# A slot-attention stage rebuilt: all sixteen batches per iteration, the recurrent cell by four, context rows streamed

## The reference, cut to what matters

```python
Pn = rmsnorm(P, input_norm_w)                 # P: the context
k_proj, v_proj = Pn @ Wk.T, Pn @ Wv.T
for _ in range(3):                            # NUM_ITERS
    sn = rmsnorm(slots, slot_norm_w)
    q_proj = sn @ Wq.T
    scores = einsum('bkd,bmd->bkm', q_proj, k_proj) * SCALE
    attn = softmax(scores, axis=-2)           # over the 56 slots
    attn = attn / (sum(attn, axis=-1) + EPS)  # over the 1500 rows
    updates = einsum('bkm,bmd->bkd', attn, v_proj)
    slots = gru_cell(updates, slots, ...)     # r, z by sigmoid, candidate by tanh
```

## Time and profile before

| | us |
|---|---|
| median of three runs | 933.5 |
| profiled execution | 936.72 |
| its span | 934.9 |
| PE busy in the span | 813.6 (87%) |
| PEld busy | 573.1 (61%) |
| DVE busy | 618.5 (66%) |
| ACT busy | 561.9 (60%) |
| POOL busy | 449.7 (48%) |

### The profile page before, as it was taken

The page is one execution under the profiler, slowest core; times in us unless marked ns, Lnnn a source line. Parts: engine busy times, 40 slices in busy tenths (PEclk is TensorE's granted clock), DMA queues, the critical chain, the costliest instruction groups (busy, mean ns, idle before and its releaser), DMA issues.

```text
span 934.9 us, 24802 instructions
## 1 busy us (share of the span) xinstructions
PE 813.6 (87%) x9152; PEld 573.1 (61%) x9152; DVE 618.5 (66%) x1210; ACT 561.9 (60%) x1222; POOL 449.7 (48%) x568
## 2 busy tenths in 40 slices
PE   5788999999999999986606899999999997599997
PEld 2254666666666666642303788899989897245443
DVE  4875777777777777614684476777677775475663
ACT  3264666666666666640442667877777875255554
POOL 1869576666666676000040135553255552066665
PEclk8798999999999999996757689999899998599999
DMA  5325444443444442201331000003320002112200
GB/s 185 84 73 167 113 132 122 124 116 117 120 121 122 120 121 50 73 2 46 99 96 49 1 2 3 2 4 99 98 71 2 2 2 68 35 35 68 68 1 20
DMA packets 44612, 66.22 MB, mean 71 GB/s; under 512 B 4964, under 2 KB 30500, under 8 KB 44532
## 3 DMA queue, kind: packets, MB, share of 16 engines
q1 hardware_dynamic: 44536, 65.21, 24.2%
HBM read 46.30 MB, written 0.46 MB: 50 GB/s over the span
## 4 chain that ended last, share of the span: by engine, by line
PE 54%; DVE 15%; POOL 15%; issue 9%; ACT 3%; DMA 2%; SPq 1%; POOLq 0%; DVEq 0%; ACTq 0%
PE ps L1220 7%; POOL ctx_lo L576 7%; PE ps L1438 7%; PE ps L1250 7%; PE ps L1237 6%; PE ps L1425 5%; PE ps L1207 3%; PE ps L1196 3%; DVE tile_max L811 2%; PE ps L1330 2%; PE ps L1254 2%; PE ps L1184 1%; POOL rs_y L566 1%; POOL rs_a L562 1%; PE ps L1175 1%
## 5 line engine op out<-in xcount | busy, mean ns | idle before, releaser
L811 DVE TENSOR_REDUCE tile_max<-ps 128x1 f32<-128x500 f32 x336 | 214.6, 674 | 74.6 <-PE ps L1220 73.9
L599 ACT ACTIVATE probs<-ps 125x896 f32<-125x896 f32 x192 | 176.1, 917 | 106.7 <-PE ps L1237 106.3
L724 ACT ACTIVATE c_prob<-ps,c_bias,row_scale 125x56 f32<-125x56 f32 x576 | 176.6, 416 | 7.2 <-DVE c_bias L1043 7.0
L1220 PE MATMUL ps<-k_hi,qdiag 128*128 128x500 f16 x336 | 130.9, 392 | 12.2 <-DVE tile_max L811 11.0
L552 POOL TENSOR_TENSOR c_prob<-c_prob,c_weight 125x672 f32<-125x672 f32 x48 | 63.0, 1312 | 155.8 <-DVE c_weight L1057 154.9
L1425 PE MATMUL ps<-query_hi,ctx_hi 128*125 128x56 f16 x576 | 109.0, 223 | 2.4 <-ACT c_prob L724 1.7
L1425 PE MATMUL ps<-query_hi,ctx_lo 128*125 128x56 f16 x576 | 110.1, 224 | 0.0
L1425 PE MATMUL ps<-query_lo,ctx_hi 128*125 128x56 f16 x576 | 110.0, 224 | 0.0
L1237 PE MATMUL ps<-qstack,kstack 98*125 98x224 f16 x768 | 108.3, 263 | 0.4 <-issue 0.2
L576 POOL TENSOR_TENSOR ctx_lo<-ctx_hi,ctx_lo 128x448 f16<-128x448 f32 x64 | 71.9, 1124 | 70.7 <-ACT ctx_lo L770 70.7
L1237 PEld LDWEIGHTS ps<-qstack,kstack 98*125 98x125 f16 x768 | 86.7, 138 | 20.0 <-issue 5.7
(11 more groups left out here) (217 smaller groups left out, 1680.3 us busy)
## 6 DMA issues: line engine op xcount, KB each, us to landing
ctx<-in_ctxT SPq DMA_DIRECT2D x16, 750.0 KB, 5.2
rows_in<-in_ctx_rows SPq DMA_DIRECT2D x16, 750.0 KB
kstack<-k_hi SPq DMA_DIRECT2D x128, 93.8 KB, 2.7
ctx_rows<-in_ctx_rows SPq DMA_DIRECT2D x16, 750.0 KB
kstack<-k_lo SPq DMA_DIRECT2D x64, 93.8 KB, 2.7
ctx_hi<-in_wg SPq DMA_DIRECT2D x8, 256.0 KB, 2.7
ctx_hi<-in_wu SPq DMA_DIRECT2D x8, 256.0 KB, 3.0
ctx_hi<-in_wd SPq DMA_DIRECT2D x8, 256.0 KB, 3.7
```

The costliest lines, as they stand in the source:

```text
L599: nc.scalar.activation(probs[c % 3][0:CH, :].rearrange("p (k w) -> p k w", k=2), score_tile(c)[0:CH], ACT.Exp, scale=float(HD) ** -0.5 / W ...
L724: last = nc.scalar.activation(c_prob[b % 4][:, c, :], ps[0:CH, 2 * (b % 2) + c // 6, bass.ts(c % 6, TOK)], ACT.Exp, bias=c_bias[b % 2][:, ...
L811: nc.vector.reduce_max(tile_max[:, u % MAXT, u // MAXT:u // MAXT + 1], ps[:, MAXB + (u + p) % 2, 0:KCOLS], AX.X).then_inc(max_done, 1)
L1220: nc.tensor.matmul(ps[:, MAXB + (u + p) % 2, 0:KCOLS], qdiag[p][:, bass.ts(t, 128)], k_hi[p][:, bass.ts(j, KCOLS)], start=True, stop=True) ...
```

## The change

The third block is restructured.

- The halves go. Each iteration runs over all 16 batches (`UNITS_C` is now 48, numbered straight through), and all loops of the stage are written out.
- The hops are for a **group of four** batches (`QUAD`, 12 groups) instead of a pair. Their tiles are 224 columns wide (`QT`) instead of 112. `update_sums` stays by pairs and stands twice per group; the root uses four spread matmuls and 128 partitions.
- The offsets are new: a group has 16 units, 64 slots, from one iteration to the next, and its last hop stands at slot 59.
- The score matmuls load 128 columns instead of 125, by reading three columns past the chunk (`ctx_hi_flat`, `ctx_lo_flat`, with `PAD` columns at the end); the three extra rows of the result are not used.
- `c_prob` has six buffers instead of four; two of them lie in memory that held weights.
- `ctx_rows` has ten tiles: four batches stay (`RESIDENT`), the other twelve are streamed through six tiles in every iteration (`STREAMED`). The source is a padded copy in DRAM, 128 rows of 12 x 129 values, contiguous per partition. In all 40 loads instead of 16, each with the norm's column rewritten by GpSimd behind it.
- The candidate and the hidden part of the gates stay in PSUM (`new_cand`, `hidden_in`) instead of going through `gru_t`.

The core of the diff:

```diff
-        TENSOR_AT = dict(sums=15, turn=18, gates=19, means=24, spread=30, project=30)
-        SCALAR_AT = dict(copy=15, tanh=16, cand=18, hi=26)
-        VECTOR_AT = dict(rows=14, hidden=19, slots=20, root=24, normed=27, lo=28)
-        POOL_AT = dict(root=19)
+        TENSOR_AT = dict(spread=55, project=59, sums=(19, 27), turn=31, gates=39, means=47)
+        SCALAR_AT = dict(copy=28, tanh=36, cand=39, hi=54)
+        VECTOR_AT = dict(rows=27, hidden=39, slots=41, root=45, normed=53, lo=57)
+        POOL_AT = dict(root=40)
...
+        def streamed_load(n):
+            it, b = divmod(n, BATCH)
+            return it * (BATCH - RESIDENT) + b - RESIDENT
...
-            for b in range(BATCH // 2):
-                sp.dma_start(ctx_rows[:, b, :, 0:D], dram["ctx_rows"][b]).then_inc(rows_loaded[b], 16)
...
+            def slot_rows(n):
+                sp.dma_start(ctx_rows_all[:, rows_of(n)], dram["ctx_rows_wide"][n % BATCH]).then_inc(rows_loaded[rows_of(n)], 16)
...
+            for b in range(RESIDENT):
+                slot_rows(b)
+            sp.wait_ge(x2_done, 2)
+            streamed = [n for n in range(UNITS_C) if n % BATCH >= RESIDENT]
+            for i, n in enumerate(streamed):
+                if i >= STREAMED:
+                    sp.wait_ge(u_ready, streamed[i - STREAMED] // 2 + 1)
+                slot_rows(n)
...
+                it, b = divmod(n, BATCH)
+                if it == 0 or b >= RESIDENT:
+                    pool.wait_ge(rows_loaded[rows_of(n)], rows_landed(n))
+                    nc.gpsimd.tensor_copy(ctx_rows[:, rows_of(n), :, D], row_sq[:, b, :]).then_inc(rms_col_done, 1)
...
+                nc.scalar.activation(new_cand, gru_t[:, 2, :], ACT.Tanh, bias=gru_b[:, 2:3]).then_inc(cand_done, 1)
...
-                        hi, lo = (x[:, batch, bass.ts(c, CH)] for x in (ctx_hi, ctx_lo))
...
-                            last = nc.tensor.matmul(ps[0:CH, 2 * (b % 2) + c // 6, bass.ts(c % 6, TOK)], l, r, start=(j == 0), stop=(j == 2))
...
+                    at = batch * CTX + c * CH
+                    hi, lo = (x[:, at:at + 128] for x in (ctx_hi_flat, ctx_lo_flat))
...
+                        last = nc.tensor.matmul(ps[:, 2 * (n % 2) + c // 6, bass.ts(c % 6, TOK)], l, r, start=(j == 0), stop=(j == 2))
```

More of the change, by code:

```diff
@@ L23 @@
 NCH = CTX // CH
+PAD = 4
 HEADS, HD = 16, 8
@@ L334, in queries_before, with quad, rows_of @@
-        def queries_before(half, it, pair):
-            return (half * (ITERS - 1) + it - 1) * PAIRS + pair + 1
+                    work(g)
+                if n < UNITS_C and unit_last:
+                    unit(n, k)
+        def quad(g):
+            return bass.ts(g % PER_IT, QT)
+        new_cand, hidden_in = (ps[:, GATES, bass.ts(i, QT)] for i in range(2))
+        def streamed_load(n):
+            it, b = divmod(n, BATCH)
+            return it * (BATCH - RESIDENT) + b - RESIDENT
+        def rows_of(n):
+            return n % BATCH if n % BATCH < RESIDENT else RESIDENT + streamed_load(n) % STREAMED
@@ new lines, in update_sums, with sums @@
+            def update_sums(pair):
+                def sums(g):
+                    m = 2 * g + pair
+                    pe.wait_ge(c_attended, 2 * m + 2)
+                    for n in (2 * m, 2 * m + 1):
+                        pe.wait_ge(rows_loaded[rows_of(n)], rows_landed(n))
+                    wait(pe, u_rows_done, g)
+                    for c in range(NCH):
+                        for j in range(2):
+                            n = 2 * m + j
+                            last = nc.tensor.matmul(ps[64 * j:64 * j + TOK, UPD, (D + 1) * pair:(D + 1) * (pair + 1)], c_prob[n % PROBS][:, c, :],
+                                                    ctx_rows[:, rows_of(n), c, :],
+                                                    start=(c == 0), stop=(c == NCH - 1), skip_group_check=True)
+                    last.then_inc(u_ready, 1)
+                return sums
@@ L1461, in slot_means @@
+            def slot_means(g):
+                pe.wait_ge(r_sq, g + 1)
+                wait(pe, qc_done, g)
+                for i in range(QUAD):
                     last = nc.tensor.matmul(ps[32 * i:32 * i + 32, QUERY, 0:TOK], ones_mean[:, 0:32], rms_sq[:, bass.ts(i, TOK)], start=True, stop=True)
                 last.then_inc(r_var, 1)
-            def spread_roots(m, k, half, pair):
-                pe.wait_ge(r_inv, 3 * k + 3)
-                wait(pe, r_slots, k)
-                for i in range(2):
-                    last = nc.tensor.matmul(ps[:, QUERY, 128 + TOK * i:128 + TOK * (i + 1)], spread[0:64, i, :], rs_y[:], start=True, stop=True)
-                last.then_inc(r_spread, 1)
@@ L1471, in project_slots, with spread_roots @@
-            def project_slots(m, k, half, pair):
-                pe.wait_ge(r_slots, k + 1)
-                wait(pe, qc_done, k)
-                nc.tensor.matmul(ps[:, QUERY, 256:256 + PT], to_query[:], slots_n, start=True, stop=True).then_inc(qc_ready, 1)
-            iterations(pe, unit_of, [(TENSOR_AT["sums"], False, update_sums), (TENSOR_AT["turn"], False, turn_updates), (TENSOR_AT["gates"], False, gate_sums),
-                                     (TENSOR_AT["means"], True, slot_means), (TENSOR_AT["spread"], True, spread_roots), (TENSOR_AT["project"], True, project_slots)])
+            def spread_roots(g):
+                pe.wait_ge(r_inv, 3 * g + 3)
+                wait(pe, r_slots, g)
+                for i in range(QUAD):
+                    last = nc.tensor.matmul(ps[:, QUERY, 64 + TOK * i:64 + TOK * (i + 1)], spread[:, i, :], rs_y[:], start=True, stop=True)
+                last.then_inc(r_spread, 1)
@@ new lines, in project_slots @@
+            def project_slots(g):
+                pe.wait_ge(r_slots, g + 1)
+                wait(pe, qc_done, g)
+                nc.tensor.matmul(ps[:, QUERY, 288:288 + QT], to_query[:], slots_n, start=True, stop=True).then_inc(qc_ready, 1)
+            iterations(unit, [
+                (TENSOR_AT["spread"], True, spread_roots), (TENSOR_AT["project"], True, project_slots),
+                (TENSOR_AT["sums"][0], False, update_sums(0)), (TENSOR_AT["sums"][1], False, update_sums(1)),
+                (TENSOR_AT["turn"], False, turn_updates), (TENSOR_AT["gates"], False, gate_sums), (TENSOR_AT["means"], True, slot_means)])
```

415 lines of the change are left out of this document (185 added, 230 removed).

## The result

The kernel after takes 880.96 us (median of 4 runs, 878.04 to 883.41) against 933.52 us of the kernel before in the same session. The ratio is 0.9448, with a 95% interval of 0.9400 to 0.9496: 52.6 us faster. The forecast was 897 us with a range from 872 to 925. The profiled execution of after took 883.04 us, its span 880.8 us.

The account below looks back on a forecast made before the run. Bound before: the cycle through GpSimd's root, beside TensorE's own load. Stage to last exponential 224.4 against 262.1 us, 37.7 less, minus 2 at its end: 36; 936.7 - 36 = 900.7, median 3.2 lower: 897 us, range 872 to 925.

Parts of the forecast that it names:

- the root cycle: Third block before: spread, score matmuls, GpSimd's root and the next pair's spread form a closed cycle, 10.74 us for two units.
- The score matmuls: TensorE, third block: with 128 columns loaded, steps fall from 57.5 to 33 ns, a unit's scores from 2.07 to 1.2 us.
- The sum to the last exponential: Third block, first to last exponential: ScalarE's exponentials, hops, waits and clock additions total 224.4 us against 262.1.
- falls of the clock: TensorE, third block: the granted clock falls once in two groups, 2 us each, 12 us in all.
- the wait of unit 3: ScalarE, fourth unit of a group: copy waits for the turn, the turn for update rows until 13.3; 0.7 us.
- The group's period: Third block: one group of four units takes 18.0 to 18.3 us, plus falls of the clock.
- The end of the stage: Behind the last exponential: the last chain stays as it is, but its hops are twice as wide, 2 us more.
- The row loads: Context row tiles, third block: 40 loads landing in 5.2 us each stay hidden; cover is gone above 6.1 us.
- ScalarE alone without falls of the clock: Rival, third block: ScalarE alone bounds it, waits shrink to some 10 us, no clock loss; 875 us, chance 0.15.
- the low-clock rival: Rival: TensorE stays at 1.2 GHz for much of the third block; 945 us, slower, chance 0.09.
- slow score matmuls: Rival, TensorE in the third block: score matmuls stay at 57.5 ns, adding 21 us; 918 us, chance 0.13.
- late rows: Rival, third block: row loads take 8.3 us each and end at 789 us; 938 us, chance 0.06.

Follow-up runs that it names:

- b_128: Kernel before with only the score matmuls' load widened to 128 columns: 927.9 us, ratio to before 0.9948.
- b_128_root1: Kernel before with score matmuls loading 128 columns and one step instead of three in GpSimd's root: 913.27 us (one run).
- a_125: Kernel after with the score matmuls loading 125 columns of context again instead of 128: 917.39 us.
- a_fill: Kernel after with eight filler matmuls of 512 columns, result unused, ahead of each turn: 870.14 us, ratio to before 0.9319.
- a_narrow: Kernel after with row tiles loaded as before, in pieces of 512 bytes instead of 6192: 946.38 us (one run).

## Why the prediction was right, and where it was off

**The bound before** was read rightly as far as the root cycle and TensorE's share of work go (b_128, b_128_root1); a third limit, VectorE's unit with a step held up beside GpSimd's attend, it did not see. The new order takes the root out of the chain but for 0.18 us in undisturbed groups, and the 128 columns are worth 36 us in it (a_125). Of the 51 us by which the stage became shorter, 17 come without the wider load (275.6 to 258.7), the other 34 with it. How the 17 divide among whole iterations, groups of four, offsets and buffers was not tested.

**The score matmuls** were taken at 33 ns; they stand 26 ns apart, about the 25 ns that the prediction had worked out for moving 56 columns alone. That this bound came out is luck. It was 0.45 ns a column, from 2.80 us over 48 update sums, and these run two at a time: in after's trace two start at 604.05, two at 604.16, two at 604.27, so 129 fp32 columns take 110 ns, 0.85 a column. By that rate 56 columns need 48 ns, and the wider load would have looked worth less than half of what was taken. The fp16 stream runs at another rate, as rows of the kernel before show: 448 fp16 columns follow each other at 190 ns (L1488 at 880.06, L1486 at 880.25), 0.42 a column. Where the columns were fp32, the same 0.45 led astray: the twelve passes of gates, forecast at 160 ns each and 2.0 us together, stand 190 ns apart and take 2.3 us. The cause given by the Trainium skill ("TensorE: Matmul & The Clock Gate", Weight-path perf modes), fast weight load with 128 weight columns and a type other than fp32, agrees with the trace: loads of 102 ns at 128 and 149 ns at 125 columns, everything else equal.

**The sum to the last exponential** was 224.4 us; it took 210.0. Term by term, for ScalarE:

| term | forecast | after |
|---|---|---|
| exponentials and hops | 170.4 + 21.0 = 191.4 | 185.4 (210.0 less the waits below) |
| tanh waits for gates, plain | 12 | 9.6 (a_fill) |
| falls of the clock | 12 | 11.4 (21.0 - 9.6) |
| copy waits for the turn | 7 | 2.3 |
| low clock at the start | 2 | 1.3 |

The 1.3 us are ScalarE's one wait for a bias in this stretch, at 538.99, behind first sums of 4.04 us; the 0.4 us in its rows above lie ahead of the first exponential and do not count here. The falls of the clock, the least certain term, came out nearly exact in sum, but partly by luck: not six falls of 2 us, but eight of nine waits for the gates longer than the undisturbed 1.2 us, by 0.3 to 2.3. The largest error (6.0 us) lies in adding rows of whole instructions: neighbours overlap. The candidate's row lasts 507 ns, but from 613.96 to the next exponential at 614.33 it holds ScalarE only 0.37 us; where nothing stands between them, 12 exponentials start 3.40 us after the 12 before, not 3.55. The second (4.7 us) is the wait of unit 3: the forecast let the update rows end 0.7 us too late for ScalarE, in the trace the copy waits 0.2 to 0.4 us. That the forecast came out 16 us too high has these causes, about 2.3 us of scatter in the first block, and small ones at the end.

**The group's period** was to be 18.0 to 18.3 us plus falls. From one group's tanh to that of the seventh group behind it (572.46 to 702.61) it is 18.6 us a group with the falls in it; in a_fill (565.61 to 686.68) 17.3, so the undisturbed period was put 0.7 to 1.0 us too high.

**The end of the stage** was to grow by 2 us. From the last exponential to L1138 it is 14.6 us against 13.5.

**The row loads** were to be hidden at 5.2 us. Their median is 5.7 us (4.0 to 11.3), and GpSimd's copies show no wait for a DMA. The bound of 6.1 us a load was not crossed on average; a_narrow shows what happens beyond it.

**The rivals.** ScalarE alone without falls of the clock (875) is what a_fill makes of the kernel (870); the low-clock rival (945) needed two thirds of the stage at the lower level, and the trace shows 0.89 on average. Its premise, that the clock falls because TensorE has idle time, is in doubt after a_125. Both bad cases were built: slow score matmuls (918) gave 917.4, by cancelling errors, and late rows (938) gave 946.4.

## What to carry to other kernels

When limits lie side by side, removing one shows little (0 and 5 us here, 20 together); such edits have to be costed and made together, and a single one that brings nothing does not prove that its target was free. An instruction that waits should stand in its queue at the slot at which its input really arrives: tanh one slot later is worth 11 us. Cost a back-to-back stream by the distance of its starts, and keep row durations for instructions that something waits for.

## What the runs showed of the hardware

- TensorE's granted clock fell again and again while the engine was busy 84% of the time with idle stretches of 2 us (after), and also while it was busy 97% with none above 0.9 us (a_125). Eight useless matmuls of 512 columns (1.89 us) in each idle stretch held it at 1.00 for all of 160 us and made the kernel 11 us faster.
- Update sums of two batches, each with 56 weight columns, start in pairs at the same time, a pair every 110 ns; 129 fp32 columns moved at 0.85 ns each, 448 fp16 columns at 0.42.
- A weight load of 125 fp16 columns instead of 128 more than doubles the distance of small matmuls, 58 ns against 26.
- A VectorE scalar_tensor_tensor with SBUF on both sides, started early in GpSimd's multiplication, ended just behind it (1.30 us for a step of 0.27). With an operand in PSUM it did not (0.39 us beside six attends).
- Row tiles in pieces of 512 bytes moved at 95 GB/s; the same tiles with 6192 bytes per partition landed in 5.7 us, and a window of 4 us in a_fill shows 358 GB/s.
